# Own row transposed and biases added by VectorE in layer 1, the carry from the last row by DMA in layer 3, and layer 0's LayerNorm by a root

## The chip, the cores and the metric

One core of a Trainium2 chip runs the whole program. The metric is device microseconds for one execution, as the median of several runs. Its engines are TensorE (PE; PEld is its loading of weights), VectorE (DVE), ScalarE (ACT), GpSimd (POOL) and SyncE (SP, here a queue that issues DMAs). Each runs its own program in order and waits on semaphores for the others.

## The reference

A graph of 10000 nodes with 512 features and 10000 edges goes through four layers; every layer takes the LayerNorm and relu of the features and adds its result to them. In float32:

```
for layer in (L0, L1, L2, L3):
    h = maximum(layernorm(x), 0)
    x = x + layer(h)
L0: twice: h = relu(segment_sum((h @ W.T + b)[src], dst))
L1: y = (1 + eps) * h + segment_sum(h[dst], src)
    y = relu(y @ W1.T + b1) @ W2.T + b2;  layernorm(y) * gamma + beta
L2: y = h + relu(h @ Ws.T + bs + mean over edges of (h[dst] @ Wn.T + bn))
    layernorm(y) * gamma + beta
L3: segment_sum(relu(concat(h[src], h[dst]) @ W.T + b), src)
```

## The kernel before, in words

Nodes and edges are padded to 10240, 80 tiles of 128. A first part sorts the edges by destination ("D") and by source ("S"). Then come five stages, one after the other, with a barrier between: layer 0's two halves (names `a_` and `b_`), layer 1 (`c_`), layer 2 (`d_`), layer 3 (`f_`). A stage goes through the 80 tiles of sorted edges. For each tile GpSimd gathers 128 rows from memory by an indirect DMA (`fetch`), and later writes 128 rows back by another (`put_rows`, a scatter). A 0/1 matrix `sel` sums the rows that belong to the same node; a sum that goes on in the next tile is carried over. Float32 products by the weights are made of three products of high and low parts (`product`: 12 matmuls of 512 columns for 512 inputs), for which ScalarE rounds the high part out of PSUM (`Thi`, `Zhi`, `Uhi`, `Hhi`, `Mhi`) and VectorE subtracts it (`Tlo` and so on).

Each engine's order is written by hand. `body(i)` lists for every place `u` of a group of four tiles (eight in layer 2) which step is done for which tile: `at(i, u, off, ...)` does the step for tile `t + off`, where `t` is the step of the loop at that place. All the engines' lists are for the same `t`, and ring buffers (`slot`) bound how far one can run ahead.

Stage `b_`: TensorE sums `t+1`, multiplies `t`, looks up indices (`pl`). VectorE does carry `t+1`, then adds the residual row `xr` (`add_x`, tile `t-1`), then `Tlo` of `t+1`, then the LayerNorm statistics of `t-1`. GpSimd gathers `b_G` and `b_xr`, raises the variances of two tiles to the power -0.5 (`make_scales`), multiplies by minus the mean (`make_biases`), and scatters the rows.

Stage `c_`: two tiles at a time. TensorE adds the own row `H` to the sum over the edges by a float32 matmul with `eye`, which is the identity times 1 + eps; the bias `b2` is a matmul of 512 columns with a matrix of ones. Stage `d_`: VectorE and GpSimd share the two LayerNorms; GpSimd adds beta to the gathered row (`keep_x`). Stage `f_`: TensorE turns the gathered rows of both ends (`turn`), multiplies (`multiply`, 24 matmuls and one for the bias), and sums the messages `Mhi`, `Mlo` by `sel`; two more matmuls with `lastsel` give the sum for the last row's node in every partition (`pc`), from which VectorE makes the carry, 128 partitions wide.

## Time and profile before

| | us |
|---|---|
| median of 3 runs | 3077.48 (3076.08 to 3077.89) |
| the profiled execution | 3067.87 |
| its span | 3065.9 |
| TensorE busy, share of the span | 2706.2, 88% |
| VectorE | 2012.9, 66% |
| ScalarE | 1231.6, 40% |
| GpSimd | 1833.0, 60% |

The profile is of one execution, which was 9.6 us below the median. Stage `b_` runs from about 784 to 1165 us of the span, `c_` from 1182 to 1818, `d_` from 1835 to 2422, `f_` from 2438 to the end. A busy TensorE is one with a matmul under way; matmuls overlap, so their cost is read from the distance between starts.

### The profile page before, as it was taken

How to read it: one execution, taken by the hardware profiler on the slowest of the kernel's cores; microseconds unless marked ns; L12 is line 12 of the kernel's file. 1: busy time of each engine (PE TensorE's matmuls, PEld its weight loads, DVE VectorE, ACT ScalarE, POOL GpSimd, SP SyncE). 2: the span in 40 equal slices, each digit the busy share in tenths (PEclk: the TensorE clock that was granted, in tenths of full speed). 3: DMA queues.
4: the chain of work that ended last, by engine and by line, in shares of the span. 5: the costliest groups of instructions: out<-in, count | busy, mean ns of one | idle time of the engine just before them, and what ended most of it. 6: DMA issues, size and time to landing. Idle time of an engine off the chain costs nothing. (4 is left out here: it accounts for less than half of the span.)

```text
span 3065.9 us, 53080 instructions
## 1 busy us (share of the span) xinstructions
PE 2706.2 (88%) x14594; PEld 2271.0 (74%) x14594; DVE 2012.9 (66%) x5558; ACT 1231.6 (40%) x2621; POOL 1833.0 (60%) x2162
## 2 busy tenths in 40 slices
PE   1279829999799996999999969999999599999998
PEld 1146518888677775999999958888888488888886
DVE  6867646665465653766666648999999555555555
ACT  0057615444455553444444424333333243333332
POOL 4657726554577775766666637776767445555553
PEclk9999999999899998999999989999999799999999
DMA  9982043333444543333333314433333244444443
GB/s 273 322 246 65 2 145 95 105 117 103 116 138 144 153 153 111 119 104 104 104 104 104 104 63 122 123 112 111 111 115 112 81 131 139 139 139 138 139 139 104
DMA packets 144688, 386.98 MB, mean 126 GB/s; under 512 B 32795, under 2 KB 33755, under 8 KB 144002
## 3 DMA queue, kind: packets, MB, share of 16 engines
q0 software_dynamic: 101408, 304.38, 33.4%
q1 hardware_dynamic: 42130, 79.44, 8.2%
q10 hardware_dynamic: 1056, 2.10, 0.2%
q8 instruction: 36, 0.59, 0.1%
q14 instruction: 58, 0.48, 0.1%
HBM read 261.22 MB, written 149.28 MB: 134 GB/s over the span
## 5 line engine op out<-in xcount | busy, mean ns | idle before, releaser
L1916 DVE SCALAR_TENSOR_TENSOR f_Mlo<-f_pm,f_Mhi 128x512 fp32r<-128x512 f32 x80 | 55.3, 692 | 263.6 <-ACT f_Mhi L1883 263.6
L803 POOL DMA_INDIRECT f_Gsrc<-rows,indexS x80 | 77.1, 964 | 217.8 <-PE f_phsrc L1955 211.9
L1883 ACT ACTIVATE f_Mhi<-f_pm 128x512 fp32r<-128x512 f32 x80 | 47.8, 598 | 376.4 <-PE f_pm L785 376.4
L1480 PE MATMUL c_pu<-c_Zhi,parts 128*128 128x256 f32 x640 | 183.2, 286 | 4.4 <-DVE c_Zlo L1403 4.4
L1482 PE MATMUL c_pu<-c_Zhi,parts 128*128 128x256 f32 x640 | 182.2, 285 | 0.0
L1649 ACT CAST d_Thi<-d_pt 128x512 fp32r<-128x512 f32 x80 | 46.9, 587 | 334.1 <-DVE d_pt L776 334.1
L1481 PE MATMUL c_pu<-c_Zlo,parts 128*128 128x256 f32 x640 | 180.6, 282 | 0.0
L1368 ACT ACTIVATE c_pu<-c_pu,c_b1col 128x256 f32<-128x256 f32 x160 | 61.8, 448 | 278.1 <-PE c_pu L1482 278.1
L807 POOL DMA_INDIRECT h<-a_rows,indexD x80 | 80.5, 1007 | 122.6 <-ACT a_rows L1061 117.8
L1469 PE MATMUL c_pt<-c_sel,c_G 128*128 128x128 f32 x640 | 124.7, 277 | 24.2 <-ACT c_H L1355 24.2
L783 PE MATMUL a_po<-parts,a_Thi 128*128 128x512 f32 x320 | 132.5, 414 | 3.5 <-DVE a_Tlo L1093 3.4
L1193 PE MATMUL b_pt<-b_sel,b_G 128*128 128x128 f32 x640 | 90.0, 285 | 48.2 <-ACT b_sel L1041 20.6
L783 PE MATMUL d_po<-parts,d_Hhi 128*128 128x512 f32 x320 | 128.9, 403 | 1.1 <-DVE d_Hlo L1673 1.1
L784 PE MATMUL b_po<-parts,b_Thi 128*128 128x512 f32 x320 | 127.5, 398 | 0.0
L784 PE MATMUL f_pm<-parts,f_Hhidst 128*128 128x512 f32 x320 | 127.4, 398 | 0.0
L783 PE MATMUL f_pm<-parts,f_Hhisrc 128*128 128x512 f32 x320 | 127.3, 398 | 0.0
L783 PE MATMUL b_po<-parts,b_Thi 128*128 128x512 f32 x320 | 127.3, 398 | 0.0
L785 PE MATMUL b_po<-parts,b_Tlo 128*128 128x512 f32 x320 | 126.9, 396 | 0.0
L785 PE MATMUL f_pm<-parts,f_Hlodst 128*128 128x512 f32 x320 | 126.8, 396 | 0.0
L785 PE MATMUL c_po<-parts,c_Ulo 128*128 128x512 f32 x320 | 126.7, 396 | 0.0
L785 PE MATMUL f_pm<-parts,f_Hlosrc 128*128 128x512 f32 x320 | 126.7, 396 | 0.0
L784 PE MATMUL f_pm<-parts,f_Hhisrc 128*128 128x512 f32 x320 | 126.4, 395 | 0.0
(458 smaller groups left out, 10045.2 us busy)
## 6 DMA issues: line engine op xcount, KB each, us to landing
rows<-n_xt SPq DMA_DIRECT2D x80, 260.0 KB, 4.0
n_xt<-in_x SPq DMA_DIRECT2D x80, 256.0 KB, 4.0
h<-q_zerorow SPq DMA_DIRECT2D x80, 256.0 KB
selrowsD<-selD SPq DMA_DIRECT2D x1, 2640.0 KB, 9.3
selrowsS<-selS SPq DMA_DIRECT2D x1, 2640.0 KB, 14.7
q_keyrowD<-in_dst POOLq DMA_DIRECT2D x1, 2560.0 KB
q_keyrowS<-in_src POOLq DMA_DIRECT2D x1, 2560.0 KB, 30.8
o_wstage<-in_L_W ACTq DMA_DIRECT2D x2, 1024.0 KB, 6.2
```

The source lines that it names most:

```text
L783: ins = pe.matmul(out, hi[:, c, :], whi[:, c, :], start=start and c == 0, stop=False)
L784: ins = pe.matmul(out, hi[:, c, :], wlo[:, c, :], start=False, stop=False)
L785: ins = pe.matmul(out, lo[:, c, :], whi[:, c, :], start=False, stop=stop and c == C - 1)
L803: return pool.indirect_dma_start(out, None, table, bass.IndirectOffsetOnAxis(ap=rows, axis=0))
L807: return pool.indirect_dma_start(table, bass.IndirectOffsetOnAxis(ap=at_rows, axis=0), rows, None, bounds_check=last_row, oob_is_err=False)
L1193: ins = pe.matmul(psum_t[s][:, c, :], G[T.slot(U)][:, c * P:(c + 1) * P], sel[s][:, :], start=True, stop=True)
L1368: ins = nc.scalar.activation(psum_u[:, c, :], psum_u[:, c, :], ACT.Relu, bias=b1col[:, c:c + 1])
L1469: pe.matmul(psum_t[s][:, c, :], G[T.slot(U)][:, cols], sel[s][:, :], start=True, stop=False)
L1480: pe.matmul(psum_u[:, o, :], g.Whi[2][:, c, cols], Zhi[:, c, :], start=c == 0, stop=False)
L1481: pe.matmul(psum_u[:, o, :], g.Whi[2][:, c, cols], Zlo[:, c, :], start=False, stop=False)
L1482: ins = pe.matmul(psum_u[:, o, :], g.Wlo[2][:, c, cols], Zhi[:, c, :], start=False, stop=c == C - 1)
L1916: dve.scalar_tensor_tensor(Mlo[s][:, :], psum_m[s][:, :], 0.0, Mhi[s][:, :].bitcast(F32), ALU.max, ALU.subtract).then_inc(s_Mlo, 1)
```

## The change

Five edits. Stage `b_`: the class `RootNorm` takes the place of `Norm`: ScalarE takes the root, VectorE divides and does one Newton step and the biases in six small instructions every other tile; GpSimd's list is one tile at a time, with `store` at -3 and `residual` at +1. Stage `c_`: ScalarE multiplies the own row by 1 + eps (`weigh`), TensorE transposes it in place of the matmul with `eye`, and VectorE adds `b2` in PSUM. Stage `d_`: GpSimd starts its gathers ahead of `keep_x`. Stage `f_`: VectorE adds `b3` in PSUM; ScalarE copies the last 32 rows of the sums, a DMA on SP's queue brings the last of them to partition 0 (`move_tail`), and VectorE does the carry on one partition. The first part loses three small VectorE steps that made `in_last` and `takes`. Preparations of the bias matrices go, too.

```diff
+    def aggregate(self, dve, tick, T):
+        dve.wait_ge(self.s_stats, T.t + 1)
+        wait(dve, self.s_bias, T.use(2) - 1)
+        dve.sem_inc(tick, 1)
+        dve.bn_aggr(self.mean_var[:, T.slot(4), :], self.stats[T.slot(2)][:, :]).then_inc(self.s_mean, 1)
+
+    def roots(self, nc, act, T):
+
+        s, h = T.slot(4), T.slot(4) // 2
+        act.wait_ge(self.s_mean, T.t + 2)
+        wait(act, self.s_bias, T.use(2) - 1)
+        nc.scalar.activation(self.root[h][:, :], self.mean_var[:, s:s + 2, 1], ACT.Sqrt, bias=self.eps[:, 0:1])\
+            .then_inc(self.s_root, 1)
+
+    def scales(self, dve, T, scales, biases):
+
+        s, h = T.slot(4), T.slot(4) // 2
+        guess, off, mean, var = (self.guess[h][:, :], self.off[h][:, :], self.mean_var[:, s:s + 2, 0],
+                                 self.mean_var[:, s:s + 2, 1])
+        n = T.use(2) * 5
+        dve.wait_ge(self.s_root, T.use(2) + 1)
+        dve.reciprocal(guess, self.root[h][:, :]).then_inc(self.s_step, 1)
+        dve.wait_ge(self.s_step, n + 1)
+        dve.scalar_tensor_tensor(off, var, LN_EPS, guess, ALU.add, ALU.mult).then_inc(self.s_step, 1)
+        dve.wait_ge(self.s_step, n + 2)
+        dve.tensor_tensor(off, off, guess, ALU.mult).then_inc(self.s_step, 1)
+        dve.wait_ge(self.s_step, n + 3)
+        dve.tensor_scalar(off, off, -0.5, 1.5, ALU.mult, ALU.add).then_inc(self.s_step, 1)
+        dve.wait_ge(self.s_step, n + 4)
+        dve.tensor_tensor(scales, off, guess, ALU.mult).then_inc(self.s_step, 1)
+        dve.wait_ge(self.s_step, n + 5)
+        dve.scalar_tensor_tensor(biases, mean, -1.0, scales, ALU.mult, ALU.mult).then_inc(self.s_bias, 1)
...
-            def scales(T):
-                s = T.slot(U)
-                ln.make_scales(pool, T, neg_half, rows[:, s:s + 2, SCALE])
-                ln.make_biases(pool, T, rows[:, s:s + 2, SCALE], rows[:, s:s + 2, BIAS])
-
...
             def body(i):
-                for pair in (0, 2):
+                for u in range(U):
+                    at(i, u, -3 if second else -2, U, NT, store)
+                    at(i, u, 4, U, NT, start_fetch)
                     if second:
-                        at(i, pair, -2, U, NT, scales)
-                    for u in (pair, pair + 1):
-                        at(i, u, -2, U, NT, store)
-                        at(i, u, 4, U, NT, start_fetch)
-                        if second:
-                            at(i, u, 2, U, NT, residual)
+                        at(i, u, 1, U, NT, residual)
...
+                        if u % 2 == 0:
+                            at(i, u, -2, U, NT, roots)
...
-                        at(i, u, -1, U, NT, finish_rows)
+                        at(i, u, -1, U, NT, aggregate_rows)
                         at(i, u, -1, U, NT, pick_node)
+                        if u % 2:
+                            at(i, u, -3, U, NT, scale_rows)
...
-                                     scale=X[s][:, SCALE:SCALE + 1]).then_inc(s_H, 1)
+                                     scale=X[s][:, SCALE:SCALE + 1]).then_inc(s_own, 1)
...
+            def weigh(T):
+                h = H[T.slot(2)][:, :]
+                act.wait_ge(s_own, T.t + 1)
+                nc.scalar.activation(h, h, ACT.Identity, scale=eps1[:, 0:1]).then_inc(s_H, 1)
...
+                        at(i, u, 6, U, NT, weigh)
...
             def norm_y(T):
+                o = psum_o[T.slot(4)][:, :]
                 dve.wait_ge(s_prod, T.t + 1)
-                ln_y.statistics(dve, T, psum_o[T.slot(4)][:, :])
+                dve.tensor_tensor(o, o, b2[:, :], ALU.add).then_inc(s_biased, 1)
+                dve.wait_ge(s_biased, T.t + 1)
+                ln_y.statistics(dve, T, o)
...
                 for c in range(C):
                     cols = slice(c * P, (c + 1) * P)
-                    pe.matmul(psum_t[s][:, c, :], G[T.slot(U)][:, cols], sel[s][:, :], start=True, stop=False)
-
-                    ins = pe.matmul(psum_t[s][:, c, :], H[s][:, cols], eye[:, :], start=False, stop=True)
+                    pe.transpose(psum_t[s][:, c, :], H[s][:, cols], g.ident[:, :])
+                    ins = pe.matmul(psum_t[s][:, c, :], G[T.slot(U)][:, cols], sel[s][:, :], start=False, stop=True,
+                                    skip_group_check=True)
...
-                pe.matmul(psum_o[T.slot(4)][:, :], ones1[:, :], b2[:, :], start=True, stop=False)
                 product(pe, psum_o[T.slot(4)][:, :], Uhi[pair][:, :, half], Ulo[pair][:, :, half], g.Whi[3], g.Wlo[3],
-                        False, True).then_inc(s_prod, 1)
+                        True, True).then_inc(s_prod, 1)
...
                 for pair in (0, 2, 4, 6):
                     at(i, pair, -2, U, NT, lengths_y)
                     for u in (pair, pair + 1):
+                        at(i, u, 5, U, NT, start_fetch)
+                    for u in (pair, pair + 1):
                         at(i, u, 2, U, NT, keep_x)
-                    for u in (pair, pair + 1):
-                        at(i, u, 5, U, NT, start_fetch)
                     at(i, pair, -2, U, NT, scales_x)
                     for u in (pair, pair + 1):
                         at(i, u, -2, U, NT, store)
...
+            def move_tail(T):
+                s = T.slot(2)
+                sp.wait_ge(s_tail, T.t + 1)
+                sp.sem_inc(tick, 1)
+                wait(sp, s_carry, T.t - 1)
+                sp.sem_inc(tick, 1)
+                sp.dma_start(tail0[s][:, :], tail[s][P - 1:P, :]).then_inc(s_tail0[s], 16)
...
-                act.wait_ge(s_msg, T.t + 1)
+                act.wait_ge(s_biased, T.t + 1)
                 wait(act, s_sum, T.t - 1)
                 nc.scalar.activation(Mhi[s][:, :], psum_m[s][:, :], ACT.Relu).then_inc(s_Mhi, 1)
...
+            def keep_tail(T):
+                s = T.slot(2)
+                act.wait_ge(s_sum, T.t + 1)
+                wait(act, s_tail0[s], 16 * T.use(2))
+                act.sem_inc(tick, 1)
+                nc.scalar.copy(tail[s][P - 32:P, :], psum_o[s][P - 32:P, :]).then_inc(s_tail, 1)
...
                     at(i, u, -1, U, NT, message)
+                    at(i, u, -2, U, NT, keep_tail)
...
-                dve.tensor_scalar(lastsel[s][:, :], ones_f[:, :], g.in_last[:, bass.ds(T.t, 1)], None, ALU.mult)
                 selection(dve, g, "S", T, sel, s_sel, s_sum)
...
+            def add_bias(T):
+                m = psum_m[T.slot(2)][:, :]
+                dve.wait_ge(s_msg, T.t + 1)
+                dve.tensor_tensor(m, m, b3[:, :], ALU.add).then_inc(s_biased, 1)
...
+            def carry_on(T):
+
+                s, before, one = T.slot(2), (T.j - 1) % 2, bass.ds(T.t, 1)
+                dve.wait_ge(s_tail0[s], 16 * (T.use(2) + 1))
+                wait(dve, s_added, T.t)
+                dve.scalar_tensor_tensor(carry[s][:, :], carry[before][:, :], g.same["S"][0:1, one], tail0[s][:, :],
+                                         ALU.mult, ALU.add).then_inc(s_carry, 1)
+
             def combine(T):
-                s, before = T.slot(2), (T.j - 1) % 2
-                one = bass.ds(T.t, 1)
-                dve.wait_ge(s_sum, T.t + 1)
+                s, before, one = T.slot(2), (T.j - 1) % 2, bass.ds(T.t, 1)
+                dve.wait_ge(s_tail, T.t + 1)
                 wait(dve, s_carry, T.t)
-                dve.scalar_tensor_tensor(carry[s][:, :], carry[before][:, :], g.same["S"][:, one], psum_c[s][:, :],
-                                         ALU.mult, ALU.add).then_inc(s_carry, 1)
-                dve.scalar_tensor_tensor(psum_o[s][:, :], carry[before][:, :], g.takes[:, one], psum_o[s][:, :],
-                                         ALU.mult, ALU.add).then_inc(s_added, 1)
+                dve.scalar_tensor_tensor(psum_o[s][0:1, :], carry[before][:, :], g.cont["S"][0:1, one],
+                                         psum_o[s][0:1, :], ALU.mult, ALU.add).then_inc(s_added, 1)
                 dve.wait_ge(s_added, T.t + 1)
                 dve.wait_ge(s_X[T.slot(U)], 16 * (T.use(U) + 1))
@@ -1934,15 +1995,15 @@
...
+                    at(i, u, -1, U, NT, add_bias)
+                    at(i, u, 1, U, NT, low)
                     at(i, u, -1, U, NT, message)
-                    at(i, u, 1, U, NT, low)
+                    at(i, u, -3, U, NT, carry_on)
                     at(i, u, -2, U, NT, combine)
                     at(i, u, 0, U, NT, select)
...
-                pe.matmul(psum_m[s][:, :], ones1[:, :], b3[:, :], start=True, stop=False)
...
-                    ins = product(pe, psum_m[s][:, :], Hhi[k][s], Hlo[k][s], g.Whi[2 + n], g.Wlo[2 + n], False, n == 1)
+                    ins = product(pe, psum_m[s][:, :], Hhi[k][s], Hlo[k][s], g.Whi[2 + n], g.Wlo[2 + n], n == 0, n == 1)
...
                 pe.matmul(psum_o[s][:, :], sel[s][:, :], Mhi[s][:, :], start=True, stop=False)
-                pe.matmul(psum_o[s][:, :], sel[s][:, :], Mlo[s][:, :], start=False, stop=True)
-                pe.matmul(psum_c[s][:, :], lastsel[s][:, :], Mhi[s][:, :], start=True, stop=False)
-                pe.matmul(psum_c[s][:, :], lastsel[s][:, :], Mlo[s][:, :], start=False, stop=True).then_inc(s_sum, 1)
+                pe.matmul(psum_o[s][:, :], sel[s][:, :], Mlo[s][:, :], start=False, stop=True).then_inc(s_sum, 1)
```

In the order of GpSimd's program in stage `b_`, before: `b_G` and `b_xr` are gathers, `rows1` a scatter.

```order
L848 TENSOR_TENSOR b_rows<-b_lnvar,b_neghalf 128x2
L854 TENSOR_TENSOR b_rows<-b_lnminus,b_rows 128x2
L807 DMA rows1<-b_rows,indexD 10241x520
L803 DMA b_G2<-h1,indexD 128x512
L803 DMA b_xr0<-in_x,indexD 128x512
L807 DMA rows1<-b_rows,indexD 10241x520
L803 DMA b_G3<-h1,indexD 128x512
L803 DMA b_xr1<-in_x,indexD 128x512
```

And the same place now. The first scatter here is of an even tile `t-3`, the gather `b_xr3` behind it is of tile `t+1`.

```order
L804 DMA rows1<-b_rows,indexD 10241x520
L800 DMA b_G2<-h1,indexD 128x512
L800 DMA b_xr3<-in_x,indexD 128x512
L804 DMA rows1<-b_rows,indexD 10241x520
L800 DMA b_G3<-h1,indexD 128x512
L800 DMA b_xr0<-in_x,indexD 128x512
```

The two small operations are gone, and each residual gather is one tile nearer to its use.

VectorE's program at an odd `t` of stage `b_` now, from `Tlo` to the next tile's `add_x` (rows that only compute a register or wait are among them).

```order
L1134 TENSOR_TENSOR b_Tlo0<-b_pt0,b_Thi0 128x512
L866 BN_STATS b_lnstats0<-b_rows 128x6
L80 ISA
L872 BN_AGGR b_lnmv<-b_lnstats0 128x2
L1177 ISA
L1177 SCALAR_TENSOR_TENSOR b_picked,b_found<-b_pl0,b_hotq0 128x128
L888 REGISTER_ALU
L889 RECIPROCAL b_lnguess1<-b_lnroot1 128x2
L890 ISA
L891 SCALAR_TENSOR_TENSOR b_lnoff1<-b_lnmv,b_lnguess1 128x2
L892 REGISTER_ALU
L893 TENSOR_TENSOR b_lnoff1<-b_lnoff1,b_lnguess1 128x2
```

Four more such rows follow it; the scales of tiles `t-3` and `t-2` are finished only behind the statistics of `t-1`.

VectorE's program in stage `f_`, one tile before.

```order
L1916 SCALAR_TENSOR_TENSOR f_Mlo1<-f_pm1,f_Mhi1 128x512
L1904 TENSOR_TENSOR f_Hlosrc1<-f_phsrc,f_Hhisrc1 128x512
L1904 TENSOR_TENSOR f_Hlodst1<-f_phdst,f_Hhidst1 128x512
L1925 SCALAR_TENSOR_TENSOR f_carry0<-f_carry1,keylastS,f_pc0 128x512
L1927 SCALAR_TENSOR_TENSOR f_po0<-f_carry1,takes,f_po0 128x512
```

The same place now.

```order
L1967 TENSOR_TENSOR f_pm1<-f_pm1,f_b3 128x512
L1958 TENSOR_TENSOR f_Hlosrc1<-f_phsrc,f_Hhisrc1 128x512
L1958 TENSOR_TENSOR f_Hlodst1<-f_phdst,f_Hhidst1 128x512
L1972 SCALAR_TENSOR_TENSOR f_Mlo1<-f_pm1,f_Mhi1 128x512
L1980 SCALAR_TENSOR_TENSOR f_carry1<-f_carry0,keylastS,f_tail01 1x512
L1988 SCALAR_TENSOR_TENSOR f_po0<-f_carry1,keyprevS,f_po0 1x512
```

The bias comes first, ahead of what ScalarE's `Mhi` waits for; `Mlo` has moved behind `Hlo`, and the carry is one tile later and one partition wide.

## Rows read from the trace of the kernel before

**Rows 1.** Four stretches, in `b_`, `c_`, `d_`, `f_`: stretch, length, busy us (instructions) of PE, PEld, DVE, ACT, POOL, clock, DMA share, GB/s.

```profile
806.00:1158.00 352.00, 324.37 (x1731) 273.36 (x1730) 214.62 (x681) 200.18 (x523) 255.80 (x300) 0.99 0.47 144
1240.00:1780.00 540.00, 540.00 (x3726) 499.20 (x3725) 348.54 (x849) 229.63 (x390) 355.89 (x387) 1.00 0.34 104
1860.00:2388.00 528.00, 527.18 (x2735) 441.62 (x2734) 490.72 (x992) 186.28 (x295) 374.29 (x402) 1.00 0.38 114
2465.00:3030.00 565.00, 565.00 (x2735) 464.22 (x2734) 317.38 (x592) 220.65 (x370) 285.41 (x295) 1.00 0.47 138
```

**Rows 2.** Timeline of stage `b_`, TensorE: start, duration, instruction; first and last of 80.

```profile
788.00 0.80 PE L1203 MATMUL b_po<-b_bstack,b_degrees 128*128 128x512 f32 x1
...
1154.67 0.48 PE L1203 MATMUL b_po<-b_bstack,b_degrees 128*128 128x512 f32 x1
```

**Rows 3.** Timeline of stage `b_`: VectorE and GpSimd; in brackets the idle time before.

```profile
920.49 0.69 DVE L1109 SCALAR_TENSOR_TENSOR b_rows<-b_po,b_xr 128x512 f32<-128x512 f32 x1
...
923.06 0.08 DVE L1132 DVE_READ_ACCUMULATOR b_picked<-b_pl,b_hotq  x1
...
926.76 0.18 DVE L835 BATCH_NORM_AGGREGATE b_lnmv<-b_lnstats 128x2 f32<-128x6 f32 x1
926.97 0.17 DVE L838 TENSOR_SCALAR b_lnvar<-b_lnmv 128x2 f32<-128x2 f32 x1
...
1150.47 1.05 POOL L807 DMA_INDIRECT rows<-b_rows,indexD  x1 [0.86 <-POOL b_rows L854]
...
1151.82 0.98 POOL L803 DMA_INDIRECT b_xr<-in_x,indexD  x1 [0.30 <-issue]
...
1155.66 0.69 DVE L1109 SCALAR_TENSOR_TENSOR b_rows<-b_po,b_xr 128x512 f32<-128x512 f32 x1 [0.83 <-issue]
```

**Rows 4.** DMA issues: count, median us from issue to landing.

```profile
b_G<-h,indexD POOLq DMA_INDIRECT x80, 3.4
```

**Rows 5.** Timeline of stage `c_`, TensorE: own row and sum (two instructions to a float32 matmul).

```profile
1501.67 0.39 PE L1471 MATMUL c_pt<-c_eye,c_H 128*128 128x128 f32 x2
1501.90 0.39 PE L1469 MATMUL c_pt<-c_sel,c_G 128*128 128x128 f32 x2
```

**Rows 6.** Timeline of stage `c_`, GpSimd: the wait at the start of a pair.

```profile
1497.90 0.72 POOL L848 TENSOR_TENSOR c_ylen<-c_lnyvar,c_neghalf 128x2 f32<-128x2 f32 x1 [1.94 <-DVE c_lnyvar L838]
```

**Rows 7.** Timeline of stage `f_`: TensorE and ScalarE, one tile.

```profile
2702.16 0.60 PE L1955 MATMUL f_phsrc<-ident,f_Gsrc 128*128 128x128 f32 x4
2702.36 0.60 ACT L1883 ACTIVATE f_Mhi<-f_pm 128x512 fp32r<-128x512 f32 x1 [4.59 <-PE f_pm L785]
2702.59 0.60 PE L1955 MATMUL f_phdst<-ident,f_Gdst 128*128 128x128 f32 x4
2702.85 0.58 ACT L1877 CAST f_Hhisrc<-f_phsrc 128x512 fp32r<-128x512 f32 x1
...
2703.50 0.39 PE L1974 MATMUL f_pc<-f_Mhi,f_lastsel 128*128 128x512 f32 x1
...
2703.73 0.40 PE L1975 MATMUL f_pc<-f_Mlo,f_lastsel 128*128 128x512 f32 x1
...
2709.81 0.60 PE L1955 MATMUL f_phsrc<-ident,f_Gsrc 128*128 128x128 f32 x4
```

**Rows 8.** Timeline of stage `f_`, VectorE: idle before `Mlo`, and a small operation.

```profile
2702.99 0.69 DVE L1916 SCALAR_TENSOR_TENSOR f_Mlo<-f_pm,f_Mhi 128x512 fp32r<-128x512 f32 x1 [3.25 <-ACT f_Mhi L1883]
...
2707.01 0.28 DVE L1910 TENSOR_SCALAR f_lastsel<-f_onesf,inlast 128x128 fp32r<-128x128 f32 x1
```

**Rows 9.** Timeline of stage `d_`: two turns that follow each other, a `keep_x` and a `sel`.

```profile
2102.11 0.60 PE L1758 MATMUL d_ph<-ident,d_H 128*128 128x128 f32 x4
...
2104.91 2.54 POOL L1586 TENSOR_TENSOR d_X<-d_X,d_beta 128x512 f32<-128x512 f32 x2
2105.16 2.38 DVE L1686 TENSOR_SCALAR d_sel<-selrowsS,keycolS,rdeg 128x128 f32 x1
...
2109.16 0.60 PE L1758 MATMUL d_ph<-ident,d_H 128*128 128x128 f32 x4
```

More of the change, by code:

```diff
@@ L897, in layer0 @@
         xr = e.ring("xr", U, [P, D], F32) if second else None
-        ln = Norm(e, "ln", True) if second else None
+        ln = RootNorm(e, "ln") if second else None
         W = None if second else Weights(nc, e, g, [(2, io.L1_W1), (3, io.L1_W2)])
@@ L1000, in _ @@
                     pool.memset(rows[:, s, BIAS + 1:EXT], 0.0).then_inc(s_const, 1)
[L1001 removed]
+            pool.wait_ge(s_const, 3 + U if second else 2)
             straight(GR, 1, 1, body, between=W and (lambda n: W.split_low(pool, n)))
@@ L1805, in layer3 @@
         Hlo = {k: e.ring("Hlo" + k, 2, [P, C, P], F32R) for k in ENDS}
-        sel, lastsel = e.ring("sel", 2, [P, P], F32R), e.ring("lastsel", 2, [P, P], F32R)
+        sel = e.ring("sel", 2, [P, P], F32R)
         Mhi, Mlo = e.ring("Mhi", 2, [P, D], F32R), e.ring("Mlo", 2, [P, D], F32R)
-        carry = e.ring("carry", 2, [P, D], F32)
+        tail, tail0 = e.ring("tail", 2, [P, D], F32), e.ring("tail0", 2, [1, D], F32)
+        carry = e.ring("carry", 2, [1, D], F32)
         rows = e.ring("rows", U, [P, D], F32)
```

99 lines of the change are left out of this document (42 added, 57 removed).

## The prediction

> **What bounds the kernel now.** I read the busy time of one stretch inside each stage first, then the timeline of one tile in each, since the five stages stand one behind the other and each can have a limit of its own. The stretches [rows 1] say which: in `c_`, `d_` and `f_` TensorE has a matmul under way all the time (540.00 of 540, 527.18 of 528, 565.00 of 565), at a granted clock of 1.00. In `b_` it has not: 324.37 of 352. The counts give the periods. A tile of `f_` issues 37 matmuls (8 turns, 4 sums, 25 products), so 2735 in 565 us are 7.64 us per tile; `d_` also has 37 and comes to 7.14; a pair of `c_` has 106 instructions (32 halves of float32 matmuls, 48, 26), so 3726 in 540 us are 15.36 us per pair; `b_` has 23 and comes to 4.68, and over all 80 tiles 366.67 / 79 = 4.64 [rows 2]. In `b_` the engine that has no rest is GpSimd: 255.80 of 352 busy, and 0.30 us before each gather or scatter, 0.86 before the one that waits for the scales [rows 3]. Two powers and biases, two scatters and four gathers fill its 9.3 us per pair. In `c_` GpSimd stands still 1.94 us per pair [rows 6], so its chain is 13.4 us long. In `f_` VectorE waits 3.25 us per tile for ScalarE's `Mhi`, which waits for the products [rows 7, 8].
>
> **Stage c_.** The own row by `eye` costs 0.23 us per 128x128 block [rows 5]. Four turns in `f_` take 0.43, so 0.108 each [rows 7]; it is the same instruction as the new transpose. Four blocks save (0.23 - 0.108) x 4 = 0.49. The bias matmul has 512 columns like those of `f_` that start 0.23 apart [rows 7]. Together 0.71 per tile, and a pair goes from 15.36 to 13.94, if TensorE stays the limit. GpSimd's chain of 13.4 still fits. VectorE has 348.54 us in 35.15 pairs, 9.92 per pair, and gets two PSUM additions of about 0.69 (the duration of `Mlo`, [rows 8]): 11.3 of 13.94. ScalarE has 6.5 and gets two copies of about 0.8: 8.1. A late addition moves the statistics by some 0.75 us, of which nothing comes back to TensorE before the next pair but one. So 0.71 x 79 = 56 less; the longer load of `b2` and the first `weigh` cost about 1. **-55**. Bounds: with a transpose as dear as the matmul only the bias is saved, -18; nothing in these rows is near that, so I take the turns' price.
>
> The Trainium skill ("TensorE: Matmul & The Clock Gate", Terms) says of the transpose mode that it is four times faster for float32; the rows above say 0.23 / 0.108 = 2.1 times. By the page a block would cost 0.058 and stage `c_` would save another 0.05 x 4 x 80 = 16 us.
>
> **Stage f_.** Three matmuls of 512 columns go, 0.23 each [rows 7]: 0.69 per tile, so 6.95 in place of 7.64, if the others keep up. VectorE has 317.38 us in 73.9 tiles, 4.29 per tile; it gets the bias (0.69), loses `lastsel` (0.28), and its two carry operations stay 512 elements long, now on one partition: 4.70. But there is a circle now: the bias must be added before `Mhi`; ScalarE then does `Mhi`, the tail, `Hhisrc`, and only then can VectorE go on with `Hlo`. ScalarE starts two copies 0.49 apart, the third takes 0.58 [rows 7]: 0.49 + 0.49 + 0.58 = 1.56. 4.70 + 1.56 + about 0.25 for handing over = 6.5 us, under 6.95. The tail's DMA has a tile's time: copied 2.1 us into the tile, needed 4.5 into the next, so 9.3 us for what takes 3.4 to 3.84 in the gathers [rows 3, 4]. It is hidden, except at the very end, where the last carry waits for it (bias 0.69, tail 0.6, the DMA, less two matmuls): +2.4. Three memsets go ahead of the first gather: about -0.8. 0.69 x 79 = 54.5, so **-53**. Bounds: -56, and -26 if the circle takes 7.3.
>
> **Stage b_.** The two powers leave GpSimd: 1.9 us of 9.3 with their waits. That alone would let the stage follow TensorE. But look at who waits for whom now. At an odd step `t` GpSimd's list is scatter `t-3`, gather `b_G`, gather `b_xr` of `t+1`. The scatter waits for the biases of the pair, which VectorE makes at the end of the same step `t`. Everything behind that scatter waits too, the residual gather among it, and VectorE needs this one in step `t+2`, ahead of `Tlo`, the statistics and the next scales. So there is a circle over two tiles, and it runs only once per two tiles:
> - six small operations, each waiting for the one before. Such starts are 0.21 apart, the last takes 0.17 [rows 3]: 5 x 0.21 + 0.17 + 0.03 = 1.25
> - from the biases to the scatter's start, as after the biases today: 0.86; the scatter and the gap 1.05 + 0.30; `b_G` and the gap 0.98 + 0.30
> - `b_xr` from its issue to the addition that waited for it: 1155.66 - 1151.82 = 3.84
> - from the start of that addition to the end of `picked`: 923.06 + 0.08 - 920.49 = 2.65
>
> Sum: 11.23 us per pair, against 9.28. Today `b_xr` is gathered one tile earlier, and the order of the pair leaves it more than a period. From the first scales on that is 38 pairs: 1.95 x 38 = 74, and the last scatters come some 1.5 us later. **+75**. TensorE, at about 8.3 per pair, isn't the limit then. ScalarE waits for a mean ahead of its root, about 2 us every other tile, beside what VectorE waits for anyway. Bounds: with the gather at its median of 3.4 [rows 4] and the gap of an unwaited scatter, 0.30, the circle is 10.2, so +37; with the small operations 0.28 apart and 0.1 more at each of the handings over, 11.7, so +94. I take the sum, since each of its terms is a row of this stage. One load of ScalarE's table stands before the first root only; it is paid once, beside this circle, and I put it at nothing.
>
> **Stage d_.** VectorE's `sel` takes 2.38 us and ends with the two `keep_x` on GpSimd [rows 9]; VectorE is busy 490.72 of 528 so it is hardly free. Turns without such a loss are 7.05 apart against 7.14 on average. With `keep_x` behind the gathers it mostly meets operations that read PSUM. At most 0.09 x 80 = 7; I take **-6**; the lower end is nothing, since TensorE hardly waits. The Trainium skill ("GPSIMD Engine Reference", Specifications) says that GpSimd's SBUF interface is shared with VectorE, with contention where VectorE is in a two-port mode or has two SBUF inputs; the row agrees, and by that page the same loss comes back if `keep_x` now meets the other `sel`, which makes this term 0.
>
> **Ahead of all.** Three small steps of about 0.24: **-0.7**.
>
> **Sum.** -0.7 + 75 - 55 - 6 - 53 = -40. The profiled execution would go from 3067.9 to 3028; the median of the runs stood 9.6 above it, so 3077.5 - 40 = 3037.5.
>
> **The rivals.**
> - The circle in `b_` doesn't close, or the gather is early enough. Then `b_` follows TensorE: 324.37 busy of 352, so -28 there and -30 over the stage. Total -145, 2933. For it: GpSimd's own load falls to 7.7 per pair. Against: the printed order, in which nothing lets `b_xr` pass the scatter.
> - The circle in `f_` is the limit at about 7.3. Then -26 there, and 3064. For it: my sum of 6.5 leaves only 0.45, and each step has more waits in the loop than before.
> - The other side: the same circle reaches 7.64 or more, by 1.1 us over my sum, if the one-partition operations or the waits around the tail cost more than the rows they replace. Then `f_` gains nothing and the total is +13, 3091. It ends slower from 7.56 us on (-7 in `f_` leaves +6). For it: two semaphores more on ScalarE and VectorE each. Against: the operations keep their length of 512.
> - A transpose of the own row costs a quarter of the matmul's 0.23 us, not half: 16 less in `c_`, 3021. The turns of `f_` speak against it. The factor is the Trainium skill's, "TensorE: Matmul & The Clock Gate", Terms.
>
> **How the numbers follow.** As forecast, with 2996 to 3073 as its own range (all bounds of `b_`, the others near their values): 0.62. `b_` follows TensorE: 0.09. `f_` at 7.3: 0.10. `f_` gains nothing: 0.11. The faster transpose: 0.04. Something else: 0.04. What the measurement can tell from no change is about 0.2%, 6 us. Slower: 0.11 and half of the last, 0.13. Same: the upper end of the first case and of the third, and half of the last, 0.07. Faster: 0.80. The range 2980 to 3080 leaves out the second case and most of the fourth.
>
> **What would show it.** The starts of the scatter in `b_` should be 11.2 apart per pair, with GpSimd waiting for VectorE's biases and VectorE's `add_x` for the gather; TensorE busy below 80% there. In `c_` pairs of 13.9 with TensorE at 100%. In `f_` tiles of 6.95, GpSimd waiting less, VectorE idle about 0.3 before the bias. In `d_` no `sel` above 1 us and turns 7.05 apart. The prediction is wrong if `b_`'s pairs are below 10 us, or if VectorE in `f_` never waits for the products.

## The result

The changed kernel takes 3032.24 us (median, 3028.79 to 3032.73), the kernel before beside it 3077.68 (3076.08 to 3079.76). The ratio is 0.9851, its 95% interval 0.9840 to 0.9863. The profiled execution took 3028.79 us with a span of 3026.9; that of before was 39.1 us longer. The profiled execution lies 3.5 us below the median now and lay 9.6 below it before, so the stages below explain 39 us, and the medians are 45 apart.

Where it went, from the first matmul of one stage to the first of the next, in us, of the two profiled executions (the forecast kept the last scatters of `b_` with `b_`, as here):

| | before | after | difference | forecast |
|---|---|---|---|---|
| up to the first matmul of `a_` | 446.7 | 450.6 | +3.9 | -0.7 |
| `a_` | 337.5 | 341.4 | +3.9 | 0 |
| `b_` | 398.2 | 461.5 | +63.3 | +75 |
| `c_` | 652.7 | 604.5 | -48.2 | -55 |
| `d_` | 602.8 | 591.9 | -10.9 | -6 |
| `f_` to the end | 628.0 | 577.0 | -51.0 | -53 |
| sum | 3065.9 | 3026.9 | -39.0 | -40 |

Four stretches of the changed kernel, one in each of `b_`, `c_`, `d_`, `f_`, with the columns of [rows 1]:

```profile
821.00:1209.00 388.00, 326.38 (x1633) 269.62 (x1633) 225.71 (x786) 195.56 (x526) 206.88 (x214) 0.95 0.41 124
1340.00:1780.00 440.00, 436.76 (x2995) 402.67 (x2994) 353.61 (x820) 247.39 (x406) 317.57 (x349) 1.00 0.37 113
1860.00:2388.00 528.00, 528.00 (x2766) 447.56 (x2766) 445.48 (x999) 201.20 (x308) 390.00 (x411) 1.00 0.39 118
2465.00:2990.00 525.00, 525.00 (x2567) 431.62 (x2566) 356.46 (x597) 275.29 (x451) 289.53 (x299) 1.00 0.52 151
```

Against [rows 1], TensorE has lost its cover only in `b_`: 84% busy, at a granted clock of 0.95. In `d_` and `f_` it still works all the time and in `c_` 99% of it, and it has less to do. The clock of `b_` falls behind its waits: behind one of 1.84 us that ends at 962.20, products start 0.43 us apart instead of 0.23 for 3.4 us. That is the lower of its levels, 1.2 GHz. In the whole of `b_` there are nine such stretches, of 3.4 or 6.8 us each.

**The circle in `b_`**, in the timeline of the changed kernel, one pair. In brackets is the idle time before, and what ended it:

```profile
953.39 0.17 DVE L899 SCALAR_TENSOR_TENSOR b_rows<-b_lnmv,b_rows 128x2 f32<-128x2 f32 x1
...
954.40 1.01 POOL L804 DMA_INDIRECT rows<-b_rows,indexD  x1 [3.15 <-DVE b_rows L899]
...
955.72 0.97 POOL L800 DMA_INDIRECT b_G<-h,indexD  x1 [0.30 <-PE b_pt L1240]
...
956.99 0.95 POOL L800 DMA_INDIRECT b_xr<-in_x,indexD  x1 [0.30 <-issue]
...
960.68 0.69 DVE L1150 SCALAR_TENSOR_TENSOR b_rows<-b_po,b_xr 128x512 f32<-128x512 f32 x1 [3.62 <-DMA b_xr<-in_x,indexD]
...
963.19 0.16 DVE L889 RECIPROCAL b_lnguess<-b_lnroot 128x2 f32<-128x2 f32 x1
...
964.20 0.16 DVE L899 SCALAR_TENSOR_TENSOR b_rows<-b_lnmv,b_rows 128x2 f32<-128x2 f32 x1
...
965.21 1.01 POOL L804 DMA_INDIRECT rows<-b_rows,indexD  x1 [3.43 <-DVE b_rows L899]
```

It is the forecast's chain link by link: biases 0.84 ahead of the scatter, 1.32 to `b_G`, 1.27 to `b_xr`, 3.69 to the addition that waits for it, 2.51 to the first small step, 1.17 for the six. Scatter to scatter is 10.81 us; the mean pair of the stage is 10.69. The waits of the stage (total, times, longest) name the same three places, GpSimd for the biases, VectorE for the residual row, ScalarE's root for the mean:

```profile
POOL rows L804 <- DVE b_rows L899: 115.4, 34, 4.0
...
DVE b_rows L1150 <- DMA b_xr<-in_x,indexD: 108.9, 33, 6.3
ACT b_lnroot L879 <- DVE b_lnmv L872: 65.7, 35, 2.9
```

**Stage `c_`**, TensorE's timeline, answers to [rows 5]: a transpose and the two-pass matmul behind it.

```profile
1509.15 0.27 PE L1510 MATMUL c_pt<-ident,c_H 128*128 128x128 f32 x1
1509.26 0.39 PE L1511 MATMUL c_pt<-c_sel,c_G 128*128 128x128 f32 x2
1509.48 0.27 PE L1510 MATMUL c_pt<-ident,c_H 128*128 128x128 f32 x1
```

0.11 us for the transpose, 0.22 for the matmul. The first products of neighbouring pairs (`c_pu`) start 13.95 and 14.00 us apart in turn, 13.98 in the mean, in place of 15.39.

**Stage `f_`**, one tile of the changed kernel: TensorE's sum, and the ring that runs over VectorE and ScalarE.

```profile
2701.53 0.49 PE L2032 MATMUL f_po<-f_Mhi,f_sel 128*128 128x512 f32 x1
...
2702.15 0.69 DVE L1967 TENSOR_TENSOR f_pm<-f_pm,f_b 128x512 f32<-128x512 f32 x1
...
2702.87 0.60 ACT L1934 ACTIVATE f_Mhi<-f_pm 128x512 fp32r<-128x512 f32 x1 [3.33 <-DVE f_pm L1967]
...
2703.49 0.58 ACT L1941 COPY f_tail<-f_po 32x512 f32<-32x512 f32 x1
...
2704.10 0.59 ACT L1928 CAST f_Hhisrc<-f_phsrc 128x512 fp32r<-128x512 f32 x1
...
2704.72 0.69 DVE L1958 TENSOR_TENSOR f_Hlosrc<-f_phsrc,f_Hhisrc 128x512 fp32r<-128x512 f32 x1 [1.88 <-ACT f_Hhisrc L1928]
...
2708.49 0.49 PE L2032 MATMUL f_po<-f_Mhi,f_sel 128*128 128x512 f32 x1
...
2709.02 0.69 DVE L1967 TENSOR_TENSOR f_pm<-f_pm,f_b 128x512 f32<-128x512 f32 x1
```

TensorE's tile is 6.96 us (7.64 in [rows 7]), and the ring takes 6.87 here. The reader is to see that VectorE's bias has no idle time ahead of it: it doesn't wait for the products, from the fourth tile on.

### The profile page after: what moved, and what is told of

It reads as the page before. It is cut to its first block and busy times, and to the rows that moved or that the text cites. A ratio compares the mean times of both kernels' runs of the same rounds, so it can differ in the third digit from the quotient of the medians.

```text
span 3026.9 us, 53029 instructions
## 1 busy us (share of the span) xinstructions
PE 2614.1 (86%) x13954; PEld 2186.8 (72%) x13954; DVE 2073.3 (68%) x5788; ACT 1360.7 (45%) x2818; POOL 1793.5 (59%) x2075
## 5 line engine op out<-in xcount | busy, mean ns | idle before, releaser
L804 POOL DMA_INDIRECT rows<-b_rows,indexD x80 | 80.7, 1008 | 160.8 <-DVE b_rows L899 136.9
L1958 DVE TENSOR_TENSOR f_Hlosrc<-f_phsrc,f_Hhisrc 128x512 fp32r<-128x512 f32 x80 | 55.3, 692 | 172.8 <-ACT f_Hhisrc L1928 172.8
L1682 ACT CAST d_Hhi<-d_ph 128x512 fp32r<-128x512 f32 x80 | 46.8, 585 | 231.8 <-PE d_ph L1796 231.8
L1150 DVE SCALAR_TENSOR_TENSOR b_rows<-b_po,b_xr 128x512 f32<-128x512 f32 x80 | 55.3, 691 | 127.6 <-DMA b_xr<-in_x,indexD 112.3
L780 PE MATMUL b_po<-parts,b_Thi 128*128 128x512 f32 x320 | 132.8, 415 | 0.0
L781 PE MATMUL b_po<-parts,b_Thi 128*128 128x512 f32 x320 | 132.0, 413 | 0.0
L1521 PEld LDWEIGHTS c_pu<-c_Zhi,parts 128*128 128x128 f32 x640 | 121.3, 190 | 13.1 <-DVE c_Zlo L1446 11.5
L780 PE MATMUL c_po<-parts,c_Uhi 128*128 128x512 f32 x320 | 129.4, 404 | 0.0
L780 PE MATMUL f_pm<-parts,f_Hhidst 128*128 128x512 f32 x320 | 127.6, 399 | 0.0
L781 PE MATMUL f_pm<-parts,f_Hhidst 128*128 128x512 f32 x320 | 126.7, 396 | 0.0
```

Source lines behind the costliest of these rows:

```text
L780: ins = pe.matmul(out, hi[:, c, :], whi[:, c, :], start=start and c == 0, stop=False)
L781: ins = pe.matmul(out, hi[:, c, :], wlo[:, c, :], start=False, stop=False)
L804: return pool.indirect_dma_start(table, bass.IndirectOffsetOnAxis(ap=at_rows, axis=0), rows, None, bounds_check=last_row, oob_is_err=False)
L1150: dve.scalar_tensor_tensor(rows[:, r, 0:D], psum_o[s][:, :], 0.0, xr[r][:, :], ALU.max, ALU.add).then_inc(s_rows, 1)
L1521: pe.matmul(psum_u[:, o, :], g.Whi[2][:, c, cols], Zhi[:, c, :], start=c == 0, stop=False)
L1958: dve.tensor_tensor(Hlo[k][s][:, :, :], psum_h[k][:, :, :], Hhi[k][s][:, :, :].bitcast(F32), ALU.subtract).then_inc(s_Hlo[k], 1)
```

## The experiments

Four chips were used. On the first, the part ahead of `a_` took 440 to 447 us in the profiles, on the other three 503 to 515, with every kernel, and the kernel before takes 3072 us on the one and 3131 to 3140 on the others. So lengths are compared by stage, which doesn't hold that part, and times by the ratio to the kernel before on the same chip. "Tile" is the mean distance of the bias matmuls (`b_po<-b_bstack`) over all 80 tiles: 4.64 us before, 5.34 after. Each kernel has one profile, so differences of a stage by 1 or 2 us are not read.

### Early residual

```diff
-                        at(i, u, 1, U, NT, residual)
+                        at(i, u, 2, U, NT, residual)
```

> The changed kernel with one number different: in stage b_ the residual row is gathered for tile t+2 again, as before, not t+1. Theory of the circle: a row gathered behind the waiting scatter is then needed three steps later and not two, so the circle of bias, scatter, b_G, b_xr, add_x, statistics, bias closes over four tiles: 0.86 + 1.35 + 1.28 + 3.84 + about 4.2 for one more tile + 2.65 + 1.25 = 15.4 us per four tiles, 3.9 per tile, under TensorE's own 4.15. The mean of 5.34 us per tile falls to 4.15 to 4.3, so b_ loses 82 to 94 us and the total is 2938 to 2950. Rival, hand-overs between VectorE and ScalarE (the root, the six small steps) hold the stage: tiles stay at 5.3 and the total at 3032. Rival, GpSimd's own load of six transfers per pair is the bound: 6 x 1.29 = 7.7 per pair, less than TensorE's 8.3, so this would show as no difference to the first theory.

Measured: 2961.69 us, ratio 0.9643 (0.9624 to 0.9663). Stage `b_` falls from 461.5 to 398.6, the tile to 4.58. `add_x` never waits for its row `b_xr` any more (109 us of waits in the stretch above). So the circle was real and this number broke it, but the stage gained 63 us and not 82 to 94: something else holds the pair at 9.2.

### Scatter last

```diff
-                    at(i, u, -3 if second else -2, U, NT, store)
+                    if not second:
+                        at(i, u, -2, U, NT, store)
                     at(i, u, 4, U, NT, start_fetch)
                     if second:
                         at(i, u, 1, U, NT, residual)
+                        at(i, u, -3, U, NT, store)
```

> The changed kernel with the residual still one tile ahead, but in GpSimd's list of stage b_ the scatter stands behind the two gathers of its tile and not ahead of them. Theory of the circle: what counts is that a gather does not stand behind the waiting scatter of the same step; the next gather of xr behind the scatter is that of the following step, needed in time: same gain as with the earlier gather, tiles of 4.15 to 4.4 us, total 2938 to 2958. Rival, it is the short distance of one tile between gather and use that costs (3.8 us of transfer in a tile of 4.15): then the tiles stay above 5 us and the total above 3015.

Measured: 2959.23 us, 0.9636 (0.9620 to 0.9652), tile 4.57. With the gather still one tile ahead, the gain is the same as with the early residual: the distance of one tile was not the cause, standing behind the scatter that waits was. The tile of 4.15 to 4.4 that was expected didn't come here either.

### Two Newton steps

```diff
+        dve.scalar_tensor_tensor(off, var, LN_EPS, scales, ALU.add, ALU.mult).then_inc(self.s_step, 1)
+        ...
+        dve.tensor_tensor(scales, off, scales, ALU.mult).then_inc(self.s_step, 1)
```

> The changed kernel with a second Newton step: four more small dependent operations of VectorE per pair of tiles in stage b_, about 0.20 us each by their starts in the changed profile, so 0.79 us per pair (the result differs from the first one only in rounding). Theory of the circle: they lie on it, so the mean pair grows from 10.69 to 11.4 and the total by 0.79 x 37 = 29 us, to 3061 (3050 to 3068). Rival, VectorE has time to spare in b_ (busy 57% there), so the stage does not feel them: 3032, within 5.

Measured: 3059.37 us, 0.9962 (0.9949 to 0.9974). Tile 5.72, stage `b_` +31.0. Four operations of 0.16 us on an engine that is 58% busy cost what their starts say, 0.76 us per pair by the tiles. They lie on the circle.

### Powers back

In stage `b_` the class `Norm` again, with GpSimd's powers and its list in pairs (one line of the edit is shown):

```diff
-        ln = RootNorm(e, "ln") if second else None
+        ln = Norm(e, "ln", True) if second else None
```

> The changed kernel with stage b_ as before alone: GpSimd's two powers and biases per pair, list in pairs, residual two tiles ahead; the edits of c_, d_ and f_ stay. Theory: b_ goes back from 5.34 to 4.64 us per tile (-55) and its last scatters come 4 us earlier, -60 in all: 2972 (2965 to 2980). The other edits are worth -39 - 60 = -99 by themselves and add up. Rival, the traces of two executions differ in b_ by something else (the clock, the memory), and the LayerNorm edit is worth less than half of it: above 3002.

Measured: 2964.16 us, 0.9653 (0.9637 to 0.9669), tile 4.64, stage `b_` 401.3. The LayerNorm edit alone cost 60 us of stage; the other edits are worth 3.5% by themselves. The time is 1 us under the range expected, on a chip where the kernel before is 6 us faster than beside the changed kernel.

### Root later

Early residual, and:

```diff
-                        if u % 2 == 0:
-                            at(i, u, -2, U, NT, roots)
+                        if u % 2:
+                            at(i, u, -3, U, NT, roots)
```

The reason for it, in the timeline of the early residual: the root comes 1.81 us late, the high part of the next tile behind it, then `Tlo`, the products, the addition, and the next mean, 9.48 us from root to root.

```profile
949.87 0.29 ACT L879 ACTIVATE b_lnroot<-b_lnmv,b_lneps 128x2 f32<-128x2 f32 x1 [1.81 <-DVE b_lnmv L872]
...
952.27 0.57 ACT L1054 CAST b_Thi<-b_pt 128x512 fp32r<-128x512 f32 x1
...
952.87 0.69 DVE L1134 TENSOR_TENSOR b_Tlo<-b_pt,b_Thi 128x512 fp32r<-128x512 f32 x1 [1.66 <-ACT b_Thi L1054]
...
953.79 0.49 PE L1250 MATMUL b_po<-b_bstack,b_degrees 128*128 128x512 f32 x1 [0.16 <-issue]
...
956.92 0.69 DVE L1150 SCALAR_TENSOR_TENSOR b_rows<-b_po,b_xr 128x512 f32<-128x512 f32 x1
...
959.35 0.30 ACT L879 ACTIVATE b_lnroot<-b_lnmv,b_lneps 128x2 f32<-128x2 f32 x1 [1.90 <-DVE b_lnmv L872]
```

> The kernel of the early residual with one step moved in stage b_: ScalarE takes the root of a pair one tile later, in the odd step, behind the high part of the sum, where the mean is long there. Theory: what is left in b_ (pairs of 9.22 us, tiles of 4.18, 4.96, 4.47, 5.05) is a second circle, on ScalarE: the root waits 1.8 us for VectorE's mean at the end of its step, the eight operations behind it and the next Thi come late, so Tlo, the statistics and the next mean. Without it b_ follows TensorE: tiles of 4.15 to 4.3 instead of 4.58, so 22 to 34 us less than with the early residual alone (2961.7 there): 2928 to 2940. Rival, GpSimd's wait for the biases (1.9 us per pair) or VectorE's small steps hold the pair at 9.2: 2962, within 4.

Measured: 3128.39 us, 0.9979 (0.9967 to 0.9991), on the second chip. Neither theory: tile 6.00, stage `b_` 509.1. Half of the tiles take 4.1 to 4.3 us, and every sixth 13.3 to 13.5 (two of them 10.4 and 10.8). This is what TensorE does in such a tile:

```profile
899.94 0.50 PE L1240 MATMUL b_pt<-b_sel,b_G 128*128 128x128 f32 x3
...
900.92 0.36 PE L1240 MATMUL b_pt<-b_sel,b_G 128*128 128x128 f32 x1 [0.48 <-issue]
...
902.34 0.36 PE L1240 MATMUL b_pt<-b_sel,b_G 128*128 128x128 f32 x1 [1.06 <-issue]
...
903.76 0.29 PEld L1240 LDWEIGHTS b_pt<-b_sel,b_G 128*128 128x128 f32 x1 [1.25 <-issue]
904.45 0.37 PE L1240 MATMUL b_pt<-b_sel,b_G 128*128 128x128 f32 x1 [1.75 <-issue]
...
905.85 0.37 PE L1240 MATMUL b_pt<-b_sel,b_G 128*128 128x128 f32 x1 [1.03 <-issue]
...
907.28 0.37 PE L1240 MATMUL b_pt<-b_sel,b_G 128*128 128x128 f32 x1 [1.06 <-issue]
```

Eight passes of one sum, between which the program has no wait, come up to 2.1 us apart. "issue" says that nothing in the trace holds them. But they aren't what the products wait for. Those come 13.4 us after the ones before them because `Tlo` is late, and `Tlo` is late because VectorE's carry is. Here are the sum that this carry waits for, the products behind it, and the carry:

```profile
895.71 1.13 PE L1240 MATMUL b_pt<-b_sel,b_G 128*128 128x128 f32 x8
...
896.59 0.48 PE L1250 MATMUL b_po<-b_bstack,b_degrees 128*128 128x512 f32 x1
...
908.19 0.22 DVE L770 SCALAR_TENSOR_TENSOR b_carry<-b_carry,keylastD,b_pt 128x4 f32<-128x4 f32 x1 [10.39 <-PE b_pt L1240]
```

The carry waits for this sum and for nothing else that is still under way, and it starts 11.6 us after the last pass of the sum. With "late" for a carry that starts over 1 us after both the last pass of its sum and the end of VectorE's own work, 25 of the 80 carries are late here, by 145 us together beyond the usual 0.42. The stage is 146 us longer than 79 tiles of 4.15 would be. In all the profiles of the first chip, of the kernel before and of the changed one no carry is more than 0.57 us after both.

Later runs ask whether it is the chip or the order.

### Aligned

Root later, and 8 unused bytes a partition (which take 32) ahead of the gathered tiles:

```diff
+        pad = e.sb("pad", [P, 2], F32)
         G = e.ring("G", U, [P, D if second else EXT], F32)
```

and the same in `f_`. That 8 bytes take 32 is the program's layout; a trace shows only what the shift does.

> The kernel with the root later, and one unused tile of 8 bytes a partition ahead of the gathered tiles in a_, b_ and f_, which moves all tiles behind it by 32 bytes, so that those that TensorE loads as weights start at a multiple of 64 bytes. Theory: a_ was 337.5 us long before and 341.1 to 342.2 in the four profiles without that tile, with the high and low matmuls 0.229 and 0.233 us apart, and 336.7 in the one where the tile was back; the place in SBUF does it. Then a_ loses 4.5 us, and f_ with 24 such matmuls a tile up to 0.0035 x 24 x 79 = 6.6: total 5 to 11 us below the kernel with the root later. Rival, the length of a_ is chance: no difference, within 3 us, and a_ at 341.

Measured: 3130.29 us, 0.9989 (0.9975 to 1.0003): not to be told from the kernel without it. By stages the theory holds in `a_` alone: 342.0 to 339.0, with sums 3.873 us apart instead of 3.912. In `f_` nothing: 577.9 and 577.6.

### Tail twice

```diff
+                wait(act, s_spare, T.t - 1)
+                nc.scalar.copy(spare[s][P - 32:P, :], psum_o[s][P - 32:P, :]).then_inc(s_spare, 1)
                 nc.scalar.copy(tail[s][P - 32:P, :], psum_o[s][P - 32:P, :]).then_inc(s_tail, 1)
```

> The changed kernel, in stage f_ with a second copy of the last 32 rows (to a tile that nobody reads) just ahead of the first, about 0.60 us more of ScalarE in every tile, between Mhi and Hhisrc. Theory from the changed profile: the circle of bias, Mhi, tail, Hhisrc, Hlo, Mlo, carry, rows, sel, bias is already 6.8 to 7.0 us long and stands beside TensorE's 6.96; with the copy it is 7.4 to 7.6 and sets the tile: + 0.45 to 0.6 x 79, less some 3 us that VectorE can fall behind, total +32 to +45 (3060 to 3073). Rival, the sum of the forecast: the circle is 6.5 long, so 7.1 with the copy: +0.14 x 79 = 11 (3039). Rival, no circle: 3028.

Measured: 3120.44 us, 0.9962 (0.9948 to 0.9976). Stage `f_` goes from 577.0 to 612.5, +35.5, as the ring of 6.9 says. Its bias additions now are 7.27 to 7.63 us apart, without idle time ahead:

```profile
2809.48 0.69 DVE L1970 TENSOR_TENSOR f_pm<-f_pm,f_b 128x512 f32<-128x512 f32 x1
...
2811.39 0.58 ACT L1944 COPY f_tail<-f_po 32x512 f32<-32x512 f32 x1
...
2817.05 0.69 DVE L1970 TENSOR_TENSOR f_pm<-f_pm,f_b 128x512 f32<-128x512 f32 x1
```

### Own row by matmul

Stage `c_` with `eye` again and without `weigh`; `b2` stays with VectorE:

```diff
-                    pe.transpose(psum_t[s][:, c, :], H[s][:, cols], g.ident[:, :])
...
+                    ins = pe.matmul(psum_t[s][:, c, :], H[s][:, cols], eye[:, :], start=False, stop=True)
```

> The changed kernel, in stage c_ with the own row by a float32 matmul with eye as before (no weigh on ScalarE); the bias b2 stays on VectorE. Theory: of the 0.705 us per tile that c_ gained, the four transposes made 4 x (0.23 - 0.11) = 0.47 and the bias matmul 0.23. So a pair is 13.98 + 0.95 = 14.93 us, stage c_ +36 less the start, where GpSimd's first pairs of 13.45 hide a part: total +30 to +36 (3058 to 3064). Rival, a transpose costs as much as a matmul and the gain is from ScalarE and VectorE order alone: +0 to +10.

Measured: 3113.67 us, 0.9944 (0.9929 to 0.9959). The pair is 14.88 us, stage `c_` 637.0. So per tile the four transposes give (14.88 - 13.98) / 2 = 0.45 us, 0.113 a block, and the bias matmul (15.39 - 14.88) / 2 = 0.25.

### Root last, root later again, residual again

On the third chip, side by side. Root last is the early residual with `roots` moved behind `hot_column`, in the same even step:

```diff
-                            at(i, u, -2, U, NT, roots)
                         at(i, u, 1, U, NT, hot_row)
                         at(i, u, 3, U, NT, sel_row)
                         at(i, u, 0, U, NT, hot_column)
+                            at(i, u, -2, U, NT, roots)
```

> The kernel of the early residual, with the root in the same even step of ScalarE as there, but as its last operation and not behind the high part; half a tile later than with the early residual, half a tile earlier than with the root later. Theory of the second circle: the root then holds back only the next high part, if the mean comes late; tiles of 4.2 to 4.4 us, 15 to 30 us below the early residual. Theory of starved instructions: when b_ goes at TensorE's own pace of 4.15 us a tile, its matmuls come 0.7 us apart now and then with nothing to wait for, as with the root later; then tiles of 5 to 6 us and a total at that of the kernel before or above the early residual by 40 us and more.

> The kernel with the root later once more, beside the early residual on the same chip. There its b_ had tiles of 6.0 us, 13.4 us between products every sixth tile, in which single matmuls of one sum started 1.4 to 2.1 us apart with no wait in the trace, while the first part of every kernel on that chip was 60 us longer. If it is the chip: here the tiles are 4.15 to 4.3 and the kernel is 22 to 34 us faster than the early residual. If it is the order of the steps: again 6.0, and 0.998 of the time before.

> The early residual once more, as the measure for the two kernels beside it. Tiles of 4.58 us in b_ in pairs of 9.2, no gap of single matmuls; ratio to the kernel before 0.964 if the chip's first part is as short as in the earlier run of it, 0.965 where it is 60 us longer. If the starved instructions come from the chip, they show here too, with tiles above 5.

Measured, against 3139.59 us: root last 0.9998 (0.9987 to 1.0009), tile 5.88; root later 0.9990 (0.9972 to 1.0008), tile 5.89; early residual 0.9832 (0.9806 to 0.9859), tile 5.26. The single passes come back with the root later, so it is no accident of one chip, and they come with the root last, too. But the early residual, which ran at 4.58 on the first chip, is slow here as well, milder: nine tiles of 79 over 7 us, where the others have one of 13.4 in every six. Only four of its sums have a pass that comes late, 0.7 to 1.4 us after the one before, and six of the nine long tiles have none. What the long tiles share is the late carry: 22 of 80 are late, by up to 5.6 us and by 67 together beyond 0.42, and each of these is followed by products that waited for its `Tlo`. That more than covers the 54 us that the 79 tiles lost against the first chip. Both theories had a part. Whether the two kernels with the root moved would be slowed on the first chip is not known; they didn't run there. Nor is it known what holds the pair of the early residual at 9.2: with the root moved, the tiles between two stalls take 4.1 to 4.3 us, as the theory of the second circle has it, but no stage without stalls shows it.

### Powers back, keep_x first

Powers back, and in `d_`:

```diff
                     for u in (pair, pair + 1):
+                        at(i, u, 2, U, NT, keep_x)
+                    for u in (pair, pair + 1):
                         at(i, u, 5, U, NT, start_fetch)
-                    for u in (pair, pair + 1):
-                        at(i, u, 2, U, NT, keep_x)
```

> The changed kernel with stage b_ as before (GpSimd's powers back) and, in stage d_, keep_x ahead of the gathers as before; the edits of c_ and f_ stay. Stage d_, read by itself: its turns were 7.09 us apart before and 7.015 after; with keep_x first they are 7.08 to 7.10 again and the stage 5 to 6 us longer than in the kernel with only the powers back (there 591.1 from its first turn to that of f_); rival, the 11 us that d_ lost come from elsewhere, then 591. Stage b_, read by itself: if the chip is one whose first part ends near 510 us and not 445, theory of starved instructions says that the old order, whose GpSimd pauses 2.7 us a pair for its powers, stays at 4.64 us a tile where the early residual fell from 4.58 to 5.26; rival, any kernel that runs b_ in under 4.7 us a tile is starved there: 5.0 to 5.3. The sum: 0.967 of the kernel before (0.9653 with the powers alone back), by the rival 0.98.

Measured, on a fourth chip: 3031.66 us, 0.9683 (0.9670 to 0.9697). Stage `d_` is 600.8 us against 591.1, its turns 7.083 apart against 7.003. Its `sel` meets `keep_x` again, as in [rows 9]:

```profile
2121.40 2.52 POOL L1629 TENSOR_TENSOR d_X<-d_X,d_beta 128x512 f32<-128x512 f32 x2
...
2121.65 2.36 DVE L1729 TENSOR_SCALAR d_sel<-selrowsS,keycolS,rdeg 128x128 f32 x1
```

Of the 74 `sel` operations from 25 us into the stage on, 37 took over 1 us before, 3 after (two in its first 125 us, one near its end), and 37 here. And stage `b_` is 399.7 with a tile of 4.63, on a chip with the long first part: the old order is not slowed, and no pass inside a sum comes late. But the carries are late here, too, 35 of 80, by up to 3.2 us:

```profile
996.96 1.13 PE L1245 MATMUL b_pt<-b_sel,b_G 128*128 128x128 f32 x8
...
1000.96 0.22 DVE L770 SCALAR_TENSOR_TENSOR b_carry<-b_carry,keylastD,b_pt 128x4 f32<-128x4 f32 x1 [2.76 <-remote]
```

The stage is no longer for it: 4.63 us per tile, as with the powers on the first chip.

## Why the prediction was right, and where it was off

The time lies 5 us under the forecast and well in its range, and the signs of the four edited stages are right. The 5 us come from the distance of the profiled execution from the median, which was taken to stay at 9.6 and is 3.5; the sum of the stages is off by 1. That it is so near is luck: two stages came 17 us under their terms together, and the other four 17 over.

**`b_`, forecast +75, measured +63.** The mechanism is as forecast: the four small operations more cost what the circle says, and the gather ahead of the scatter and the earlier gather each take it away, down to 4.57 and 4.58 per tile. The step that was off is its length, 11.23 us per pair, where it measured 10.81 in the pair shown: the gather took 3.69 and not 3.84, the stretch behind it 2.51 + 1.17 and not 2.65 + 1.25. All 79 tiles together are 422.2 us long, 55.5 more than before, where the forecast had 74. TensorE is 84% busy there, where less than 80% was named as a sign. The last scatters end the stage 4.3 us later, and not 1.5; the other 3.5 of the 63 lie ahead of the first matmul of `c_`, put at 1. The first `weigh` has a part in it: without it (own row by matmul) they are 2.1. That the longer load of `b2` is the rest is not shown. The rival in which `b_` follows TensorE was wrong twice: even with the circle broken the tile stays at 4.57 to 4.58 and not 4.15.

**`c_`, forecast -55, measured -48.** The price of the transpose and of the bias was right to 0.04 us per tile. The steady pairs give 39 x 1.41 = 55. What is missing is the start, put at 1 us: three of the first six pairs take 15.58, 15.70 and 17.41 us, where before only one was longer than the steady 15.39 (16.94). The likely reason is that GpSimd, which stands still 1.94 us per pair before and 0.53 to 0.56 now, has less time to make up for a late beginning; no run tests that. The rival of the cheap transpose is out: 0.11 us is half of the matmul's 0.23. The Trainium skill ("TensorE: Matmul & The Clock Gate", Terms) gives a factor of four there, and the runs show 2.

**`d_`, forecast -6, measured -11.** The turns gave 5.8 of it (7.089 to 7.015 us), as forecast, though the 7.14 that was read from the counts is 7.09 by the turns themselves. The other 5 lie in the end of the stage and the start of `f_`. With the order put back, 9.7 of the 11 come back, 6.3 of them in the turns. The other 3.4 were not in the forecast: the last scatter starts 23.4 us after the last turn with the gathers first and 26.8 with `keep_x` first. `keep_x` doesn't slow another `sel` in its place.

**`f_`, forecast -53, measured -51.** TensorE's 0.69 per tile came in full in the steady tiles (7.65 to 6.96). Yet the forecast of VectorE's slack failed: it should have been idle 0.3 us ahead of the bias and wait for the products, and by its own words the prediction is wrong where VectorE never does. It does in the first three tiles only, and in none of the 77 behind them. The ring is 6.8 to 7.1 us long and not 6.5: ScalarE's three steps follow each other 0.61 apart and not 0.49 (1.85 for 1.56), and the rest takes 5.02 for 4.95; where its starts are 7.05 or 7.09 apart, the remainder was not followed up. VectorE falls 0.04 us per tile behind TensorE, and 80 tiles are too few for that to count. The rival with a ring of 7.3 was nearer than its chance of 0.10: one more copy makes it 7.5.

**Ahead of `b_`, forecast -0.7, measured +7.8.** The first 3.9 are within what the four profiles on the first chip differ by in this part, 440.0 to 447.4, though it is the same in all four. Of the 3.9 of `a_`, 3.1 are the place of its tiles (0.039 x 79, below). Both together are as large as the error in any other stage but `b_`, and no term of the forecast had them.

The kernel to keep is that with GpSimd's powers back in `b_` and the other edits kept: 0.9653. On the first chip scatter last (0.9636) and early residual (0.9643) tie with it. Early residual reached only 0.9832 on the third chip, where the powers with `keep_x` first reached 0.9683 on the fourth. The two were not run side by side on such a chip, and scatter last not at all.

## What to carry to other kernels

Work that is taken off an engine's list leaves its waits there: look at what stands behind the waiting instruction, and follow it round until it meets itself; the length of that ring per turn is the price, whatever the engines' busy shares say. A gather that would stand behind an instruction that waits goes ahead of it, or is started a tile earlier; here one number was worth 63 us. Where an edit on the bounding engine succeeds, work out the ring that comes next, since it may stand 0.1 us behind.
